# A state-space scan and an expert layer on one core: a two-part fp32r stack, plain matmuls for the sum over the states, and reordered routing, head and tail

## The reference, cut to what matters

```
u      = silu(causal_conv4(in_proj @ ctx) + conv_b)              # 256 channels
B, C   = rows of x_proj @ u                                      # 16 states each
delta  = softplus(dt_proj @ dt_lo + dt_b)
state  = state * exp(delta * A) + (delta * u) * B                # per channel, 16 states
y      = (sum over states of state * C + D * u) * silu(layernorm(x))
x      = x + y.T
```

```
probs = softmax(xn @ Wg); the two largest; place = number of earlier tokens with this expert
kept if place < 320; out = sum of gate * (relu(rows @ w1[e]) @ w2[e]); x = x + out
```

## Time and profile before

| | |
|---|---|
| median of 3 runs | 352.02 us (350.09 to 355.56) |
| profiled execution | 351.8 us, its span 350.0 us |
| busy | TensorE 257.1, VectorE 247.2, GpSimd 214.4, ScalarE 167.3 us |
| mean granted TensorE clock | 0.816 |
| first scan starts | 22.86 us |
| gate_y of the last batch starts | 189.05 us |
| first expert matmul | 211.61 us |

### The profile page before, as it was taken

The page is one execution under the profiler, slowest core; times in us unless marked ns, Lnnn a source line. Parts: engine busy times, 40 slices in busy tenths (PEclk is TensorE's granted clock), DMA queues, the critical chain, the costliest instruction groups (busy, mean ns, idle before and its releaser), DMA issues. The chain is left out here.

```text
span 350.0 us, 4871 instructions
## 1 busy us (share of the span) xinstructions
PE 257.1 (73%) x1508; PEld 232.2 (66%) x1508; DVE 247.2 (71%) x397; ACT 167.3 (48%) x355; POOL 214.4 (61%) x168
## 2 busy tenths in 40 slices
PE   8756264875708828356653599999999999999970
PEld 7535154754607627245652498899999999999970
DVE  1498986999997898999995055466567585857610
ACT  1479424775424944255314026364747465463710
POOL 0494745985960779726915018548677777768642
PEclk9696856898657885656756569999999999999996
DMA  7754410007000083001105205635554545464110
GB/s 169 228 167 137 196 48 0 0 2 267 6 0 0 32 301 98 24 0 47 45 0 176 74 1 180 220 121 170 216 187 149 186 148 189 154 243 166 80 50 34
DMA packets 14641, 39.45 MB, mean 113 GB/s; under 512 B 2794, under 2 KB 9628, under 8 KB 11712
## 3 DMA queue, kind: packets, MB, share of 16 engines
q1 hardware_dynamic: 11360, 32.23, 27.4%
q0 software_dynamic: 2816, 6.32, 4.9%
q10 hardware_dynamic: 448, 0.70, 0.8%
HBM read 31.81 MB, written 8.47 MB: 115 GB/s over the span
## 5 line engine op out<-in xcount | busy, mean ns | idle before, releaser
L328 POOL TENSOR_TENSOR dbu<-du,bsb 128x1024 f32<-128x1024 f32 x31 | 72.4, 2354 | 11.2 <-DVE h L1109 5.4
L1109 DVE TENSOR_TENSOR_SCAN h<-ps,dbu 128x1024 f32<-128x1024 f32 x32 | 73.1, 2284 | 3.6 <-ACT ps L504 3.3
L504 ACT ACTIVATE ps<-delta,anegs 128x255 f32<-128x255 f32 x128 | 53.0, 462 | 34.8 <-DVE h L1109 31.0
L700 PE MATMUL ps<-stack,sels 96*128 96x256 bf16 x80 | 19.3, 338 | 67.6 <-DVE hc L1120 64.9
L700 PEld LDWEIGHTS ps<-stack,sels 96*128 96x128 bf16 x80 | 6.7, 109 | 75.7 <-issue 71.2
L1270 DVE SCALAR_TENSOR_TENSOR htlo<-ps,hthi 128x320 fp32r<-128x320 f32 x64 | 30.5, 487 | 35.6 <-ACT hthi L624 21.3
L730 PE MATMUL ps<-cst,hc 128*128 128x128 f32 x256 | 48.5, 352 | 2.1 <-DVE hc L1120 2.1
L730 PEld LDWEIGHTS ps<-cst,hc 128*128 128x128 f32 x256 | 43.4, 189 | 3.6 <-DVE hc L1120 2.3
L404 POOL TENSOR_TENSOR w2lo<-w2raw,w2hi 128x512 fp32r<-128x512 f32 x30 | 38.3, 1300 | 10.9 <-ACT w2hi L615 10.7
L895 PE MATMUL ps<-xthi,w1hi 128*128 (+1 forms) x128 | 40.1, 313 | 0.4 <-issue 0.4
L895 PE MATMUL ps<-hthi,w2hi 128*128 128x320 f32 x128 | 40.3, 315 | 0.0
(11 more groups left out here) (143 smaller groups left out, 501.6 us busy)
## 6 DMA issues: line engine op xcount, KB each, us to landing
w1raw<-in_w SPq DMA_DIRECT2D x8, 1024.0 KB
w2raw<-in_w SPq DMA_DIRECT2D x8, 1024.0 KB
bsb<-b_rows SPq DMA_DIRECT2D x6, 1024.0 KB, 6.0
expert_rows<-fill SPq DMA_DIRECT2D x1, 2580.0 KB, 10.5
xe<-expert_rows SPq DMA_DIRECT2D x8, 258.0 KB
out<-x SPq DMA_DIRECT2D x4, 256.0 KB, 5.2
sels<-in_sel SPq DMA_DIRECT2D x1, 768.0 KB, 10.8
xnat<-in_x SPq DMA_DIRECT2D x1, 768.0 KB, 11.4
```

What stands on the lines that cost most here:

```text
L328: nc.gpsimd.tensor_tensor(dbu[j % DRING][:], du[:, :, None, cols(b)].to_broadcast([P, EC, 2, L]), bsb[b % 2][:, None, 2 * p:2 * p + 2, :]. ...
L504: ins = nc.scalar.activation(decays(g % SLOTS_DA)[:, c, i * L + 1:(i + 1) * L], delta[:, c, b * L + 1:(b + 1) * L], ACT.Exp, scale=anegs[: ...
L1109: nc.vector.tensor_tensor_scan(h[g % HRING][:].rearrange("p c n t -> p (c n t)"), decays(g % SLOTS_DA).rearrange("p b t -> p (b t)"), dbu[ ...
```

## The change

- The stack has two fp32r parts, 64 rows, and `lo_rows` is one subtraction from PSUM. The one-hot rows are a 64x32 table that is read with a step of zero; it arrives in brow and ScalarE copies it, first in its queue, behind a wait.
- Only two `b_cast` remain; the rest of batch 0's B goes over DRAM as for the later batches (`spread_b(0)`), ahead of the 2580 KB fill of the experts' rows.
- `add_state` does plain fp32 matmuls with the identity, no longer with the transpose flag.
- `drive(j)` waits through `quiet` for mult(j-5) and the small work behind it.
- `choose` and `place` read the logits and counts from PSUM; some operations are merged; `choose`, `place` and `send` come earlier, in the last batch by more.
- The softplus for batch 1 comes one step earlier.
- Head: fewer keep_clock ahead, seven in the middle, delta's projection ahead of that of B and C. Tail: turn and logits come ahead of the wait for expert 0's rows, 8 keep_clock in place of 16, `low_w1` of expert 0 ahead of `choose`.

The core of the diff ("..." stands for lines left out):

```diff
-XPC = 3 * BC
+XPC = 2 * BC
...
+CASTS = 2
...
-        sels = sm("sels", [XPC, BC * P], BF16)
-        stack = sm("stack", [XPC, T], BF16)
-        rest = sm("rest", [XPC, L])
-        brow = sm("brow", [DS, L])
+        sels = sm("sels", [XPC, BC], F32R)
+        stack = sm("stack", [XPC, T], F32R)
+        brow = sm("brow", [XPC, L])
...
-            sp.dma_start(sels[:], sel).then_inc(s["sel_in"], 16)
+            sp.dma_start(brow[0:XPC, 0:BC], sel).then_inc(s["sel_in"], 16)
...
+                for name, n0, n1 in (("b_lo_in", 0 if b else 2 * CASTS, PAIRS), ("b_hi_in", PAIRS, DS)):
+                    sp.dma_start(bsb[b % 2][:, n0:n1, :], b_dram[b:b + 1, n0:n1, :].to_broadcast([P, n1 - n0, L])
                                  ).then_inc(s[name], 16)
...
+            spread_b(0)
+            sp.wait_ge(s["fill_made"], 1)
+            sp.dma_start(xe_dram.rearrange("(t p) r -> p t r", p=P),
+                         fill[:, None, :].to_broadcast([P, SLOTS // P, ROW])).then_inc(s["xe_filled"], 16)
             spread_b(1)
...
+            def quiet(g):
+
+                b, p = divmod(g, PAIRS)
+                pool.wait_ge(s["mult_done"], g + 1)
+                if b == 0 and p == 3:
+                    pool.wait_ge(s["z_stats"], 2)
+                if b == 0 and p == 6:
+                    pool.wait_ge(s["z_scale"], 2)
+                if b >= 1:
+                    if p == (1 if b == B - 1 else 2):
+                        pool.wait_ge(s["ln_var"], b)
+                    if p == (3 if b == B - 1 else 5):
+                        pool.wait_ge(s["ln_scale"], b)
+                    if p == (4 if b == B - 1 else 6):
+                        pool.wait_ge(s["gates_done"], b)
...
-                if b == 0:
+                if j < CASTS:
                     pool.wait_ge(s["b_done"], j + 1)
                 else:
-                    pool.wait_ge(s["b_lo_in" if p < PAIRS // 2 else "b_hi_in"], 16 * b)
-                if j >= DRING:
-                    pool.wait_ge(s["scan_done"], SLOTS_DA + j - DRING + 1)
+                    pool.wait_ge(s["b_lo_in" if p < PAIRS // 2 else "b_hi_in"], 16 * (b + 1))
+                if j == DRING:
+                    pool.wait_ge(s["scan_done"], SLOTS_DA + 1)
+                if j > DRING:
+                    quiet(j - DRING - 1)
...
-                    if p == 4:
-                        softplus_d(1)
-                        softplus(1)
-                        delta_u(1)
+                if b >= 0 and b + 1 < B and p == 3:
+                    softplus_d(b + 1)
+                    softplus(b + 1)
+                    delta_u(b + 1)
...
-                    if p == 1 and b >= 2:
-                        if b == 2:
+                    if p == 7:
+                        if b == 1:
                             pool.wait_ge(s["xe_filled"], 16)
-                        send(b - 2)
+                        send(b - 1)
...
-                act.wait_ge(s["top_sub"], b + 1)
-                nc.scalar.activation(etop[:, tiles_of(b), :], etop[:, tiles_of(b), :], ACT.Exp
-                                     ).then_inc(s["top_exp"], 1)
+                act.wait_ge(s["top_bias"], b + 1)
+                for j in range(b * BT, (b + 1) * BT):
+                    ins = nc.scalar.activation(etop[:, j, :], top[:, j, :], ACT.Exp, bias=ntop[:, j:j + 1],
+                                               scale=rx[:, j:j + 1])
+                ins.then_inc(s["top_exp"], 1)
...
+            act.wait_ge(s["sel_in"], 16)
+            nc.scalar.activation(sels[:], brow[0:XPC, 0:BC], ACT.Copy).then_inc(s["sel_done"], 1)
             act.wait_ge(s["wdt_psum"], 1)
             nc.scalar.activation(wdt[:], ps[:, YBANK, :].rearrange("p (k d) -> p k d", k=EC), ACT.Copy
...
-            hi_rows(0, BBANK)
             decay_exps(0, V0BANK)
+            hi_rows(0)
+            act.wait_ge(s["sel_done"], 1)
+            b_rows(0)
+            logs(0)
             b_copy(0)
-            logs(0)
             b_copy(1)
...
-            b_copy(2)
...
-                if g + 3 < PAIRS:
-                    b_copy(g + 3)
...
-                    ins = nc.tensor.matmul(ps[:, bank, i * L:(i + 1) * L], sels[:, (n0 + i) * P:(n0 + i + 1) * P],
+                    n = n0 + i
+                    ins = nc.tensor.matmul(ps[:, bank, i * L:(i + 1) * L], sels[:, n:n + 1].to_broadcast([XPC, P]),
                                            stack[:, cols(b)], start=(i == 0), stop=True, skip_group_check=True)
...
-                                                   stop=(g % PAIRS == PAIRS - 1), is_transpose=True,
-                                                   skip_group_check=True)
+                                                   stop=(g % PAIRS == PAIRS - 1), skip_group_check=True)
                 return ins
...
-                pe.wait_ge(s["multi_done"], b + 1)
-                pe.wait_ge(s["lg_done"], b + 1)
+                pe.wait_ge(s["oh_done"], b + 1)
...
+                nc.tensor.matmul(before, onesf[0:1, :], cst[0:1, CBASE:CBASE + BT * NE].rearrange("p (t e) -> p t e", e=NE),
+                                 start=True, stop=False, skip_group_check=True)
+                for k in range(TOPK):
+                    last = nc.tensor.matmul(before, tri[:], oh[:, tiles_of(b), k, :], start=False, stop=False,
+                                            skip_group_check=True)
+                    for t in range(1, BT):
+                        last = nc.tensor.matmul(before[:, t:BT, :], ones[:], oh[:, b * BT:(b + 1) * BT - t, k, :],
+                                                start=False, stop=False, skip_group_check=True)
+                    for j in range(b * BT):
+                        last = nc.tensor.matmul(before, ones[:], oh[:, j:j + 1, k, :].to_broadcast([P, BT, NE]),
+                                                start=False, stop=False, skip_group_check=True)
                 last.then_inc(s["pos_psum"], 1)
...
-            keep_clock(11, V0BANK)
+            keep_clock(5, V0BANK)
...
+            keep_clock(7, BBANK)
+            pe.wait_ge(s["wdt_done"], 1)
+            for k in range(EC):
+                pe.wait_ge(s["u_done"], k + 1)
+                ins = dt_part(0, k, V0BANK)
+            ins.then_inc(s["v_psum"], 1)
+
+            def project(b):
+                for c in range(EC):
+                    ins = x_proj(b, c, BBANK)
+                ins.then_inc(s["xp_psum"], 1)
...
-                    ins.then_inc(s["xp_psum"], 1)
-                ins = dt_part(0, c, V0BANK)
...
+            pe.wait_ge(s["sel_done"], 1)
             pe.wait_ge(s["stack_done"], 1)
+            pe.wait_ge(s["brow_done"], 1)
             b_cast(0)
-            pe.wait_ge(s["wg_done"], 1)
-            c_cast(0)
             b_cast(1)
             pe.wait_ge(s["ctx_in"], 16)
             pe.wait_ge(s["cw_done"], 1)
             conv(1, 0, YBANK)
-            b_cast(2)
+            pe.wait_ge(s["wg_done"], 1)
+            c_cast(0)
             conv(1, 1, YBANK)
-            b_cast(3)
...
-                if g + 4 < PAIRS:
-                    b_cast(g + 4)
...
+                if nb < B and p == 1:
+
+                    pe.wait_ge(s["u_done"], EC * (nb + 1))
+                    if b < 2:
+                        pe.wait_ge(s["b_done"], CASTS)
+                    else:
+                        pe.wait_ge(s["slots_done"], b - 1)
+                    project(nb)
+                    dt_bias(WBANK)
+                    dt_part(nb, 0, WBANK)
+                    dt_part(nb, 1, WBANK).then_inc(s["v_psum"], 1)
                 if p == 5:
...
+            pe.wait_ge(s["slots_done"], B - 1)
             pe.wait_ge(s["scan_done"], SLOTS_DA + STEPS)
+            keep_clock(4, DABANK)
+            turn_x1(B - 1)
+            keep_clock(4, DABANK)
+            logits(B - 1)
             pe.wait_ge(s["xe_in"], 32)
             place_rows(0)
-            pe.wait_ge(s["pos_done"], B - 1)
-            turn_x1(B - 1)
+            counts(B - 1)
             place_rows(1)
-            logits(B - 1)
-            keep_clock(8, CBANK)
-            counts(B - 1)
-            keep_clock(8, CBANK)
-            pe.wait_ge(s["pos_done"], B)
+            pe.wait_ge(s["slots_done"], B)
...
-                link(nc.vector.tensor_tensor(rest[:], ps[0:XPC, bank, 0:L], stack[:, bs], ALU.subtract))
-                nc.vector.tensor_copy(stack[BC:2 * BC, bs], rest[BC:2 * BC, :])
-                link(nc.vector.tensor_copy(stack[2 * BC:3 * BC, bs], rest[2 * BC:3 * BC, :]))
-                nc.vector.tensor_tensor(stack[2 * BC:3 * BC, bs], rest[2 * BC:3 * BC, :],
-                                        stack[2 * BC:3 * BC, bs], ALU.subtract
+                dve.wait_ge(s["brow_done"], b + 1)
+                nc.vector.tensor_tensor(stack[BC:2 * BC, cols(b)], ps[BC:2 * BC, BBANK, 0:L],
+                                        stack[BC:2 * BC, cols(b)].bitcast(F32), ALU.subtract
                                         ).then_inc(s["stack_done"], 1)
...
```

(45 more changed lines are left out.)

164 lines of the change are left out of this document (39 added, 125 removed).

## The result

The changed kernel takes 330.27 us (median of 4 runs, 325.98 to 331.69), the kernel before 351.64 us beside it; the ratio is 0.933, 95% interval 0.921 to 0.945. That ratio is of the fast runs alone (for the changed kernel 325.98 and 329.18), since the other two, 331.36 and the profiled 331.69, lie more than 1.5% above the fastest. The forecast was 328.1. The profiled execution of the changed kernel took 331.7 us with a span of 329.9, and 20.1 us of span have gone.

| us | before | after | change | forecast |
|---|---|---|---|---|
| start to first scan | 22.86 | 22.88 | 0 | -2.5 |
| first scan to last gate | 166.2 | 156.1 | -10.1 | -11.6 |
| last gate to first expert matmul | 22.6 | 13.1 | -9.5 | -9.6 |
| experts | 138.4 | 137.9 | -0.5 | 0 |

What follows compares the result with a forecast made beforehand. VectorE, stretched beside GpSimd's products, was taken to bound the scan stage, with the head and tail chains of waits. 351.8 - 11.6 (scan stage) - 9.6 (tail) - 2.5 (head) = 328.1 us; range 318 to about 341.

Steps and rivals of the forecast that it cites:

- the head: Start to first scan: fewer fillers and removed load traffic start the first scan between 0 and 5 earlier; -2.5 us taken.
- the tail: Behind the last gate: turn no longer waits for expert 0's rows, fewer fillers, `low_w1` moved; -9.6 us, bounds -7 and -11.
- item 5: Scan stage, TensorE: plain sums take 16 records, not eight; +4.0 in batches 1 and 2, +1.9 and +1.0 last; +6.9 us.
- Item 1: Scan stage, VectorE: one `lo_rows` from PSUM replaces the two subtractions and two casts of `parts`; -9.6 us.
- Item 2: Scan stage, batch 1's softplus a step earlier: wait for ScalarE's exp goes, -4.9; GpSimd late +3.2, `lo_rows(1)` waits +2.1 us.
- Item 3: Scan stage, `choose`: three contending instructions remain of six, GpSimd drains three products in place of four; together -6.1 us.
- Item 4: Scan stage, `place`: the wait of 1.80 for the copy of the counts goes, with less arithmetic; together -3.2 us.
- Item 6: Scan stage: fp32r row layout, fewer `b_cast`, six ScalarE copies gone, `quiet` waiting for mult; nothing on the path.
- D: Rival, chance 0.1: reordering fails, GpSimd late for the ring in every batch, `choose` collides as before; 339, twice that 346.
- Rival A: Chance 0.2: plain sums in the scan stage cost no more than now, or the clock stays high; 321 us.
- B: Rival, chance 0.08: TensorE becomes the bound of the scan stage, slower than before; 381 us if its level stayed low.
- C: Rival, chance 0.12: gain of head and tail lost to late transfers of one-hot table and expert 0's rows; 337 us.

Runs made afterwards that it cites:

- e1_flag: The changed kernel with the transpose flag back on the sums over the states; 323.17 us, ratio 0.916 to the kernel before.
- e2_noquiet: The changed kernel with GpSimd's ring waiting for the scan as before, without the waits for small work; 329.3 us, ratio 0.931 to the kernel before.
- e4_clock: The changed kernel with four filler calls of TensorE behind each half of the last batch's placing calls; 327.88 us, ratio 0.935 to the kernel before.
- e7_quiet_early: The changed kernel with GpSimd waiting for `choose` two products earlier in batches 1 and 2; 329.3 us, ratio 0.934 to the kernel before.
- e10_flag_last: The changed kernel with the transpose flag in the last 8 of the 32 sums alone; 327.33 us, ratio 0.929 to the kernel before.
- e11_flag_rest: The changed kernel with the transpose flag in the first 24 sums alone, plain sums in the last batch; 325.69 us, ratio 0.927 to the kernel before.

## Why the prediction was right

Right in sign and in most of its mechanism. The forecast is 2.2 us under the median; in the profiled execution it is 3.6 under, 2.5 of it from the head, 1.5 from the scan stage and 0.1 from the tail, less 0.5 of the experts. Part of the closeness is luck: two totals below, item 5 and the tail, are right over parts that are not. By its steps:

- **Item 1, stack.** -9.3 against -9.6, and `lo_rows(1)` waited 1.3 where 2.1 was forecast.
- **Item 2, softplus.** -4.9 and +3.3, as computed (-4.9, +3.2). The number of GpSimd's operations between two points, each at its duration, against VectorE's steps between them, was enough.
- **Item 3, `choose`.** -7.6 with its waits against -6.1. That VectorE drains GpSimd's products was right, their number was not: oh fell into the change between two products in batch 1, where one stretched instruction was left in place of three; in batch 2 two were left, oh with 1.93 and ntop with 2.35. In batch 3 the 1.0 saved went into the wait for the logits.
- **Item 4, `place`.** -2.5 against -3.2: the wait of 1.80 is gone, but ohc, now earlier, was stretched to 0.95 in batch 1.
- **Item 5, plain sums.** +6.8 against +6.9, and e1_flag confirms it. The total was right, its parts were not: 2.0 in the first three batches (0.7 to 2.2 over several executions) against 4.0, 4.5 to 4.9 in the last against 2.9. VectorE's waits there were named, except that for the logits. The records, 2.05 and 3.78 us a sum, were foreseen from `open_sums` (2.1 and 3.9).
- **Item 6.** Nothing for the waits of `quiet`: e2_noquiet bears it out. What I put down as free and was not is the variance of batch 3, 2.48 in place of 0.17, because VectorE now reaches it beside a product (+2.3); it starts at 148.67 and ends at 151.15, with GpSimd's product at 151.11. The size of small work changes when its neighbours move, as the forecast said of `choose` only.
- **Tail.** -9.5 against -9.6, out of two errors that cancel. To the slots it was 11.0, not 9.6, since the logits came without a wait behind `low_w1`; behind them the product with the gathered rows ran at the low level, 4.55 in place of 2.32 before, which e4_clock gives back.
- **Head.** Here a step failed: "Between 0 and 5 earlier; a late table costs up to 3. I take -2.5." In the profiled execution it was 0. Seven traces with this head have their first scan between 20.2 and 24.0, on average 22.2, against 23.0 in three traces of the old one: -0.8. The step took GpSimd's queue for the path, as running without a gap from 12.97 to 22.77; but it waits 1.72 in between for VectorE, and the first scan starts right behind VectorE's own queue in both kernels. These are rows of the kernel before, GpSimd and then VectorE:

```profile
18.32 0.84 POOL L299 TENSOR_TENSOR rz<-vz,nhalf 128x2 f32<-128x2 f32 x1 [1.72 <-DVE vz L1026]
...
21.54 1.23 DVE L1095 TENSOR_TENSOR dbu<-du,bsb 128x1024 f32<-128x1024 f32 x1
22.68 0.15 DVE L1030 SCALAR_TENSOR_TENSOR nmz<-mvz,rz 128x2 f32<-128x2 f32 x1
```

The gain is there and is lost again: VectorE's last product ahead of the scan starts at 19.30 in place of 21.54, 2.2 earlier, and nmz behind it takes 2.31 in place of 0.15, because GpSimd's first product now runs from 19.80 on. The loads do come earlier, as the forecast had it (GpSimd starts on cwb at 9.16 in place of 12.97). In some executions the head also stands at the low level; that the fewer fillers do this is not proved.

One sum of the recorded text is off: with D's terms taken twice the time is 328.1 + 2 x 10.6 = 349 and not 346. The range did not rest on it.

Rival A is refuted, by the flag in both kernels. B was far from deciding: the clock rose to 0.81 to 0.95. C did not happen: the rows of expert 0 were there. D's collision of `choose` was smaller than before; e7_quiet_early shows it as a matter of where the collision lies. That most of the plain sums' price lay in the last batch of this kernel is shown by e10_flag_last; why the wait for the logits left in e11_flag_rest is open.

## What to carry to other kernels

Cost a slower instruction in the place with the least cover, and anew for each order of the queues: in the changed kernel the last 8 of 32 sums had most of the price, at three waits of one batch, and the 24 others cost 2 us or less in their own batches; in the kernel before, the last 8 had 1.8 of 4.4. A small instruction costs what runs beside it on the shared port, so moving it or GpSimd's work changes its price, and to hold GpSimd back at one place only moved the collision (7.95 us against 7.92). Read a change of 1 or 2% by stage from several traces: the head alone spread by 4 us between executions of the same head.

## What the runs showed of the hardware

- A 128x128 fp32 matmul with the identity is one record with the transpose flag and two without: eight calls take 1.04 and 2.05 us at the high level, 1.91 and 3.78 at the low. The flagged form is the cheaper one for a sum, although the granted clock is lower with it (0.71 against 0.88 of full speed from 23 to 175 us).
- A tensor_scalar on 128x2 numbers took 2.48 us beside a product of GpSimd and 0.17 without: with one input it is not free of the stretching that the two-input operations show.
- The same instructions in the first 12 us ran at either of the two levels from run to run (the 14 fillers' records 1.83 to 3.36 us), with no difference in the code ahead of them: 3.35 in e10_flag_last, 1.83 in e1_flag.
